# Constant products ahead of the score pairs of an induced-attention phase, on one Trainium2 core

## What is computed

```python
def _mha(q, k, v, in_w, in_b, out_w, out_b):
    wq, wk, wv = jnp.split(in_w, 3, axis=0)
    bq, bk, bv = jnp.split(in_b, 3)
    qh = (q @ wq.T + bq).reshape(q.shape[0], q.shape[1], NH, HD)   # NH 8, HD 16
    ...
    scores = jnp.einsum('bqhd,bkhd->bhqk', qh, kh) / jnp.sqrt(jnp.asarray(HD, qh.dtype))
    attn = jax.nn.softmax(scores, axis=-1)
    o = jnp.einsum('bhqk,bkhd->bqhd', attn, vh).reshape(q.shape[0], q.shape[1], D)
    return o @ out_w.T + out_b
...
ind_b = jnp.broadcast_to(ind, (x.shape[0], M, D))      # M 128, D 128
h = _mab(ind_b, x, x, p1)
return _mab(x, h, h, p2)
...
h = h + _L0_attn_ref(_layernorm(h, axis=-1), ...)
```

## Time and profile before

| | |
|---|---|
| runs, device time | 2368.10, 2378.34, 2375.04 us; median 2375.04 us |
| profiled execution, device time | 2374.71 us |
| its span, first to last instruction | 2372.9 us |
| mean granted clock of TensorE | 0.884 of full speed |
| busy over the span | PE 86%, DVE 56%, ACT 49%, POOL 33% |
| `induce` | about 1342 to 1930 us of the span |
| `experts` | from about 1930 us |

### The profile page before, as it was taken

How to read it: one execution, slowest core, us unless ns; L and a number is a source line. 1 busy time by engine, 2 the same in 40 slices (tenths; PEclk the granted TensorE clock), 3 DMA queues, 4 the chain that set the end, 5 groups by cost and what they waited for, 6 DMA issues and landing times. The chain is left out here.

```text
span 2372.9 us, 44240 instructions
## 1 busy us (share of the span) xinstructions
PE 2032.6 (86%) x14601; PEld 1459.1 (61%) x14601; DVE 1337.5 (56%) x4495; ACT 1159.1 (49%) x2495; POOL 780.1 (33%) x975
## 2 busy tenths in 40 slices
PE   5799999999999999999998468887778429999986
PEld 4466666666666656666665346665545229999972
DVE  2365656555655566565664245667676615555547
ACT  2476666666666566666664014454444214444434
POOL 0012222122212121222212211123577845555546
PEclk7799999999999999999998656787776559999995
DMA  3641343034412442133400223422321167777644
GB/s 101 125 74 16 64 68 67 29 42 68 68 42 27 91 68 53 22 63 68 66 4 1 62 63 82 99 54 58 67 59 42 49 220 230 227 232 226 204 150 142
DMA packets 113988, 207.11 MB, mean 87 GB/s; under 512 B 23076, under 2 KB 47654, under 8 KB 113112
## 3 DMA queue, kind: packets, MB, share of 16 engines
q1 hardware_dynamic: 102616, 184.90, 34.6%
q0 software_dynamic: 10176, 17.09, 2.1%
q10 hardware_dynamic: 976, 2.30, 0.3%
HBM read 147.59 MB, written 64.66 MB: 89 GB/s over the span
## 5 line engine op out<-in xcount | busy, mean ns | idle before, releaser
L679 ACT ACTIVATE tower_prob<-tower_prob,tower_negmax 128x386 f32<-128x386 f32 (+1 forms) x768 | 390.4, 556 | 304.3 <-DVE tower_negmax L886 303.6
L886 DVE CUSTOM_DVE_ANT_0 tower_prob<-tower_sbank,tower_band 128x386 f32<-128x386 f32 (+1 forms) x768 | 346.2, 488 | 139.9 <-PE tower_sbank L453 134.7
L491 PEld LDWEIGHTS tower_tbank<-tower_ident,tower_prob 128*128 128x128 f32 x1920 | 228.2, 143 | 130.0 <-issue 81.2
L491 PE MATMUL tower_tbank<-tower_ident,tower_prob 128*128 128x128 f32 x1920 | 284.5, 279 | 22.9 <-DVE tower_probT L911 21.2
L735 ACT ACTIVATE tower_probT<-tower_tbank 128x384 f32<-128x384 f32 (+1 forms) x576 | 227.5, 430 | 126.7 <-PE tower_tbank L491 124.6
L2052 POOL DMA_INDIRECT scratch_yt<-experts_y,experts_rows x190 | 186.7, 983 | 184.6 <-DVE experts_y L2195 153.9
L430 PE MATMUL tower_dbank<-tower_oxT,tower_w 96*128 96x512 f32 x384 | 191.5, 624 | 13.0 <-ACT tower_oxT L724 12.9
L2110 PE MATMUL experts_ybank<-experts_w,experts_hid 128*128 128x128 f32 x1520 | 185.3, 275 | 0.0
L2098 PE MATMUL experts_hbank<-experts_zT,experts_w 128*128 128x256 f32 x760 | 183.5, 385 | 1.1 <-ACT experts_zT L2134 1.1
L453 PE MATMUL tower_sbank<-tower_k_st,tower_q_st 49*128 49x386 f32 (+1 forms) x768 | 161.0, 413 | 26.2 <-POOL tower_k_st L635 14.0
L2110 PEld LDWEIGHTS experts_ybank<-experts_w,experts_hid 128*128 128x128 f32 x1520 | 177.5, 192 | 0.1
(11 more groups left out here) (314 smaller groups left out, 3473.7 us busy)
## 6 DMA issues: line engine op xcount, KB each, us to landing
experts_w<-ew SPq DMA_DIRECT2D x95, 578.0 KB
scratch_qk<-tower_qk SPq DMA_DIRECT2D x64, 384.0 KB, 4.6
tower_q_st<-scratch_qk SPq DMA_DIRECT2D x96, 192.0 KB, 7.5
tower_k_st<-scratch_qk SPq DMA_DIRECT2D x96, 192.0 KB, 10.4
experts_rows<-scratch_zs SPq DMA_DIRECT2D x95, 132.0 KB
scratch_kq<-induce_kq SPq DMA_DIRECT2D x8, 1024.0 KB, 4.3
experts_res<-scratch_yt SPq DMA_DIRECT2D x8, 1024.0 KB, 6.7
induce_k_st<-scratch_kq SPq DMA_DIRECT2D x48, 128.0 KB, 4.2
```

Source lines behind the costliest of these rows:

```text
L491: mm = pe.transpose(bank[:, jb * P:jb * P + P], prob[:, hg % PR, at + jb * P:at + jb * P + P], ident[:, :])
L679: act.activation(prob[:, hg % PR, 0:width(i)], prob[:, hg % PR, 0:width(i)], ACT.Exp, bias=negmax[:, hg % PR:hg % PR + 1], scale=-1.0).the ...
L886: scores.copied(dve.tensor_tensor_reduce(prob[:, hg % PR, 0:width(i)], bank[:, 0:width(i)], band[:, BAND_AT[i]:BAND_AT[i] + width(i)], sca ...
```

## The change

A helper `stay_warm` is called at the four places where a pair of score banks has been claimed, before the scores are computed. It issues two products of a stationary matrix of ones with `upper`, which is read four times over, so that each has 512 columns; both go to the first claimed bank with `start=True`, and the scores that follow overwrite them. Nothing reads them. PE also waits for the `late` constants once more, at step 0, since `upper` is one of them. No other engine's stream is changed.

```diff
+        WARM = 2
...
+            def stay_warm(bank):
+
+                for _ in range(WARM):
+                    pe.matmul(bank[:, :].rearrange("p (t c) -> p t c", c=P), allones[:, :],
+                              upper[:, :].rearrange("p (t c) -> p t c", t=1).broadcast_to([P, NT, P]),
+                              start=True, stop=True)
...
                     banks = [scores.claim(pe, ("s1", m, head)) for head in heads]
+                    stay_warm(banks[0])
...
                     banks = [scores.claim(pe, ("s2", m, head)) for head in heads]
+                    stay_warm(banks[0])
...
                     banks = [turned.claim(pe, ("t1", m, head)) for head in heads]
+                    stay_warm(banks[0])
...
                     banks = [turned.claim(pe, ("t2", m, head)) for head in heads]
+                    stay_warm(banks[0])
...
                 if g == S1[0]:
                     pe.wait_ge(o_clear, 1)
+                    pe.wait_ge(late_in, LATE)
```

## The result

The change takes 2382.01 us (median of 20 runs, 2379.01 to 2387.35) against 2375.93 us for the kernel before (20 runs, 2368.10 to 2380.89, the three shown ahead of the prediction among them). The profiled execution has a span of 2382.0 us.

The account below looks back on a forecast made before the run. PE was taken to bound 1387 to 1648, POOL the part behind. Added 51 us, less 28 saved and 9 to 10 hidden, zero behind 1648: 2374.7 + 13 = 2388 us, range 2340 to 2425.

Parts of the forecast that it names:

- the band of no change: Whole kernel: a time within 12 us (about 0.5%) of the kernel before, either way; chance 0.26.
- PE is the bound, cold and warm: In 1387 to 1648, PE sets the pace cold; warm, it shares it with the chains through DVE and ACT.
- Half the time is cold; the calls bring the cold share to 0.2: In 1387 to 1648: about 130 us cold at a clock of 0.75; likeliest cold share afterwards 0.2, clock 0.90.
- A call costs 0.50 warm, 0.85 cold: Price in us of one call of two products, behind the claim of the score banks.
- Added 51, saved 28, hidden 9 to 10: In 1387 to 1648, 90 calls at a cold share of 0.2, in us: 13 to 14 us longer.
- the term for the saving: In 1387 to 1648: cold work made warm saves 47 x (1 - s/0.5) us, s being the cold share of time.
- Zero behind 1648: After 1648: the 38 calls change nothing, as POOL paces the steps; ends a 40 us gain, a 24 us loss.
- The pause stays and brings the clock down: Where PE waits for a bank, the 5.32 us DMA or DVE, pauses stay as long and lower the clock.
- The case without response: Rival: in 1387 to 1648 s stays at 0.5; 2425 us, or 2449 with calls behind 1648 uncovered; chance 0.10.
- The warm case: Rival: in 1387 to 1648 s falls to 0.05 or below; 2350 us; decided at a clock of 0.96; chance 0.31.
- The signs named ahead: 1387 to 1648: clock 0.85 to 0.92, PE busy at least 220 us; first scatter 1660 to 1675, first to last 274.
- The wait for `late`: At step 0: PE's second wait for these constants costs nothing, as they land at 1358, before the first scores at 1387.2.

Follow-up runs that it names:

- The second profile of the change: The unmodified change measured again on another chip, against the kernel before: ratio 1.0026; the profiled execution had a span of 2373.3 us.
- the wait alone: The change without its products, only the second wait for the late constants, against the kernel before: 2388.53 against 2390.75 us, ratio 0.998.

## Why the prediction was right, and where it was not

The sign, the mechanism and the range held: slower, by 6 us of the 13 forecast, within 2340 to 2425. The sign owes something to luck: the forecast was a net of 13 us between terms of 51 and 28, and the terms missed by nearly as much as the net. And 6 us lie inside the band of no change, to which I had given 0.26, less than the 0.43 for slower beyond it.

- **PE is the bound, cold and warm.** Shown: two more products that hold no clock cost 71 us on top of the change (the clock fell to 0.82 with them), and two more that do hold it cost 20, on other chips.
- **Half the time is cold; the calls bring the cold share to 0.2.** Measured 0.24, a clock of 0.88 where I had 0.90.
- **A call costs 0.50 warm, 0.85 cold.** Measured 0.54 and 0.94 to 0.98. The second way of costing, half a float32 product with 0.49 and 0.94, was right for the cold clock. The Trainium skill ("TensorE: Matmul & The Clock Gate", Part 1) has 215.7 and 426.7 ns from start to start, by which a call is an estimated 0.43 and 0.85 us. The trace shows a tenth of a us more a call. It agrees for products in a row: four in a call take 0.97 us warm (1540.67 to 1541.64 in the run with four), 0.43 more than two do.
- **Added 51, saved 28, hidden 9 to 10: here the sum was off, and the saving is the term that was mis-sized.** From 45.6 us behind the start of the phase to the first scatter, before and after:

```profile
1387.00:1655.00 268.00, 218.12 (x1571) 152.40 (x1571) 169.92 (x501) 118.21 (x220) 57.99 (x89) 0.74 0.35 72
```

```profile
1391.22:1662.30 271.08, 235.25 (x1748) 141.75 (x1749) 170.95 (x501) 118.41 (x219) 58.09 (x88) 0.89 0.37 71
```

PE is busy 17 us longer and idle 14 us less. To part the 17 us, I count each PE instruction of the two traces from its start to the start of the next, or to its own end where PE then idles. The products take 56 us (41 warm, 15 cold), and all other work takes 179 where it took 218. So 56 were added, 39 saved and 14 hidden, which gives the loss of 3 us. The term for the saving gives 28, and 24 at s = 0.24. It was too small for two reasons. The ratio of warm to cold was taken from one group as 0.6; over all groups of the phase that ran more than five times in each clock before the change it is 0.53, and L1100 in the earlier trace rows has 0.97 to 1.87, which is 0.52. And the other work that ran cold fell from 123 to 41 us, to a third and not to s/0.5, a half, since the products themselves take 15 of the 62 us that are still cold. The second profile of the change gives 53 added, 45 saved and 13 hidden. The run with one-row products, against the wait alone, gives 68 added, nothing saved (3 us more of other work) and 21 hidden: there nearly a third of the price vanished in idle time.
- **Zero behind 1648, because POOL sets the pace.** The number was right, the reason wrong. With one-row products that part grew by 22 us, close to the 24 I gave as its upper end. It is zero because its clock rose too (0.70 to 0.90 and 0.66 to 0.75), and without the late calls and without that clock the time is the same. With four products a call first to last takes 280.6 us (1682.8 to 1963.4), against 279.4 with none on that chip.
- **The pause stays and brings the clock down.** The pauses stayed, but with products around them they no longer always bring it down. PE waits 3.4 us for the same signal of DVE in both kernels. Before:

```profile
1636.33 2.05 PE L1095 MATMUL induce_dbank<-induce_wout,induce_o2T 128*128 128x128 f32 x8 [3.39 <-DVE sh_count L1761]
1638.17 1.91 PE L1237 MATMUL induce_dbank<-induce_l,induce_hid 128*128 128x128 f32 x8
```

and after:

```profile
1645.92 1.13 PE L1096 MATMUL induce_dbank<-induce_wout,induce_o2T 128*128 128x128 f32 x8 [3.38 <-DVE sh_count L1774]
1646.89 1.06 PE L1249 MATMUL induce_dbank<-induce_l,induce_hid 128*128 128x128 f32 x8
```

The same groups run at half clock behind the pause before, at full clock after. In the second profile of the change a cold stretch of 3.4 us follows this pause, so it is not sure to be ridden out. In the front part, with fewer items under way, the clock still falls at the 4.94 us before T1 and three more times, some 30 us apart, the last time up to 1517.9. Where products filled the pause of item 0 in part, it fell all the same; where they closed the pause of item 1, little of what follows was cold (0.91 against 0.50). What that is worth in time is open.
- **The rivals.** The case without response is what the one-row products do, and its upper price, 2449 us, is what they give (2376 x 1.0306 = 2449). The warm case has its crossing at a clock of 0.96 by my sum; in the one execution with 0.93 (2375.12 us) the change ran level with the kernel before (2377.54), which suggests that the crossing lies lower, as the larger saving makes it.
- **The signs named ahead.** A clock of 0.88, PE busy 226 us and 276 us from the first to the last scatter are as forecast; a warm pair is just above its 0.4 to 0.5. The first scatter, at 1662.3, is in the forecast's 1660 to 1675 only with the 4.2 us from before the phase.
- **The wait for `late`** costs nothing, as forecast.

## What to carry to other kernels

Products without a use can raise the granted clock, and here gave back 67 us, but they are paid for on the same engine. Where PE is the bound in both clocks, work out the two sides separately before hoping for the sum. Put them where the engine waits anyway: between two claims they probably cost 5 us less than behind both. Price a saving in the clock from all groups that run cold and not from one. To measure the price alone, run the same count and columns with operands of one row.

## What the hardware showed that I had not expected

Products of 512 columns on one row of the array take as long as on 128 rows (0.96 us a pair cold, 0.53 warm) but left the clock where it was: 0.70 in 1387 to 1648, against 0.73 with no products on the same chip. On 128 rows the same count gave 0.88. A pause of 3.4 us that was followed by half clock in the kernel before was followed by full clock in the change. And one kernel's clock varies from execution to execution (0.88 and 0.93 in this stretch) by as much as one product a call moved it, with 8 us of time up to the first scatter.
